# Selective-scan block with mixing and table FFN on one core: where the next group's weights are transposed

## The reference, cut to what matters

```
proj = einsum('bld,pd->blp', h, in_proj_w)            # 10304 x 512 weights
gate, hbc, dt = split(proj)
xBC = silu(causal_conv_4_taps(hbc))
x, B, C = split(xBC)                                  # 64 heads of 64, 8 groups, state 128
state_t = state_{t-1} * dA_t + dt_t*x_t (outer) B_t ; y_t = state_t . C_t     # 32 steps
y  = y + x * D
yn = y * rsqrt(mean(y*y over the 512 channels of a group) + eps) * norm_weight * silu(gate)
out = einsum('bli,di->bld', yn, out_proj_w)           # 512 x 4096 weights
```

## Time and profile before

| | |
|---|---|
| median of 3 runs | 3331.55 us |
| profiled execution, its own time | 3330.75 us |
| its span, first to last instruction | 3329.0 us |
| mean granted TensorE clock | 0.997 |
| TensorE matmuls busy | 3293.0 us (99%) |
| VectorE busy | 2609.7 us (78%) |
| ScalarE busy | 1765.0 us (53%) |
| GpSimd busy | 738.1 us (22%) |
| DMA queue of SP | 464.72 MB, 41.2% of 16 engines |

### The profile page before, as it was taken

One profiled execution on the slowest core, in us unless ns is written; L12 is line 12 of the kernel. 1 busy time (PEld: TensorE's weight loads), 2 busy tenths in 40 slices (PEclk: granted clock), 3 DMA queues, 4 the chain that ended last, 5 costly groups with the idle time before them and its releaser, 6 DMA issues. The chain is left out here.

```text
span 3329.0 us, 86577 instructions
## 1 busy us (share of the span) xinstructions
PE 3293.0 (99%) x33306; PEld 2735.0 (82%) x33306; DVE 2609.7 (78%) x4367; ACT 1765.0 (53%) x3203; POOL 738.1 (22%) x520
## 2 busy tenths in 40 slices
PE   8999999999999999999999999999999999999999
PEld 6778788888888888888888888888888888888888
DVE  6787878888888888888888888888888878887443
ACT  5666665555555555555555555555555545554111
POOL 1122212222212222112222112222122221222333
PEclk9999999999999999999999999999999999999999
DMA  7433354334533364334443363435433542225331
GB/s 276 161 112 114 139 186 161 106 134 168 187 118 126 114 225 140 120 126 169 159 139 137 115 213 109 139 139 180 155 119 120 181 159 79 99 78 157 98 90 60
DMA packets 207793, 466.29 MB, mean 140 GB/s; under 512 B 35134, under 2 KB 80606, under 8 KB 198284
## 3 DMA queue, kind: packets, MB, share of 16 engines
q1 hardware_dynamic: 206364, 464.72, 41.2%
q0 software_dynamic: 368, 0.85, 0.1%
q10 hardware_dynamic: 1024, 0.27, 0.0%
HBM read 313.68 MB, written 152.09 MB: 140 GB/s over the span
## 5 line engine op out<-in xcount | busy, mean ns | idle before, releaser
L1155 PE MATMUL low_banks<-ht,wt 128*128 128x512 f32 x6144 | 1423.4, 390 | 9.3 <-DVE xc L1404 9.3
L1155 PEld LDWEIGHTS low_banks<-ht,wt 128*128 128x128 f32 x6144 | 1153.6, 188 | 258.6 <-DVE xc L1404 13.1
L1404 DVE SCALAR_TENSOR_TENSOR xc<-low_banks,cvw,xc 128x496 f32<-128x496 f32 (+2 forms) x1152 | 824.0, 717 | 221.1 <-ACT xc L1294 193.2
L1250 PE MATMUL bank<-wot,gy 128*128 128x512 f32 x3072 | 729.7, 393 | 1.2 <-DVE gy L1446 1.2
L1250 PEld LDWEIGHTS bank<-wot,gy 128*128 128x128 f32 x3072 | 567.2, 188 | 129.1 <-DVE wnext L1440 10.6
L1294 ACT ACTIVATE xc<-low_banks,cvb,cvw 128x512 f32<-128x512 f32 x384 | 298.6, 780 | 497.6 <-PE low_banks L1155 497.5
L1092 POOL TENSOR_TENSOR r<-rv,neg_half 128x4 f32<-128x4 f32 x64 | 98.4, 1537 | 1767.2 <-DVE rv L1494 1767.2
L1155 PE MATMUL bank<-ht,wt 128*128 128x512 f32 x1536 | 387.3, 401 | 0.0
L1155 PEld LDWEIGHTS bank<-ht,wt 128*128 128x128 f32 x1536 | 280.2, 189 | 55.8
L1073 POOL TENSOR_TENSOR segr<-adts,mask_le 128x1024 fp32r<-128x1024 f32 x128 | 243.1, 1921 | 351.8 <-DVE adts L1395 351.8
L1273 ACT ACTIVATE xc<-xc 128x512 f32<-128x512 f32 x384 | 241.1, 628 | 140.1 <-DVE xc L1404 139.4
(11 more groups left out here) (195 smaller groups left out, 3444.4 us busy)
## 6 DMA issues: line engine op xcount, KB each, us to landing
ht<-h_d SPq DMA_DIRECT2D x63, 2048.0 KB, 8.9
acc_d<-acc SPq DMA_DIRECT2D x64, 1024.0 KB, 4.3
wt_d<-wnext SPq DMA_DIRECT2D x112, 512.0 KB, 9.4
acc<-acc_d SPq DMA_DIRECT2D x56, 1024.0 KB, 7.0
wt<-wt_d SPq DMA_DIRECT2D x70, 512.0 KB, 6.6
stage<-in_L_attn_in_proj_w SPq DMA_DIRECT2D x84, 256.0 KB, 2.7
wot<-wt_d SPq DMA_DIRECT2D x28, 512.0 KB, 8.0
xb<-in_x SPq DMA_DIRECT2D x8, 1024.0 KB, 8.4
```

Source lines behind the costliest of these rows:

```text
L1155: ins = pe.matmul(pb[:, :], wt[:, n, l, k, :], ht[:, rr, k, :], start=(q == 0 and k == 0), stop=(q == 2 and k == KC - 1))
L1250: ins = pe.matmul(bank[OUT[t]][:, :], gy[:, c, l, t * P:(t + 1) * P], wot[:, rr, c, :], start=(c == 0 and q == 0), stop=(c == CT - 1 and q ...
L1404: ins = dve.scalar_tensor_tensor(dst, src, cvw[:, n, TAPS - 1 - k:TAPS - k], dst, ALU.mult, ALU.add)
```

## The change

The next group's weights are no longer transposed by TensorE. In pass `it`, ScalarE splits each raw chunk of 512 32-bit numbers a row into two planes of 16-bit halves (`halves`, laid over the part of `gy` that channel tile 2 uses later), SP issues one transposing DMA for each chunk (`turned`, laid over the low parts' place in `wnext`), and in pass `it + 1` GpSimd joins the halves again in `stage`, ScalarE copies the high parts after its first tap, and GpSimd subtracts for the low parts; then SP stores them and loads the next raw chunks. ScalarE may not overwrite `halves` until the DMAs are done, so it waits for them before `high(2)`. The 14 chunks go through in seven passes, and the eighth moves no raw chunk. TensorE has one loop for all groups. In the first group ScalarE's sort of x is gone: VectorE's addition reads x from z at a step of 4 elements.

```diff
@@ line 890 of before @@
+    halves = [nc.alloc_sbuf_tensor_at(f"halves{u}", [P, 2, DM], U16, offset=gy_at + 8 * TT * HG * L + 4 * DM * u) for u in range(2)]
+    turned = [nc.alloc_sbuf_tensor_at(f"turned_halves{u}", [P, 2 * KC, P], U16, offset=sh.wnext_at + 8 * DM * u + 4 * DM) for u in range(2)]
...
@@ line 983 of before @@
-def next_chunks(j):
-    return 2 + j, (j % 2 if j < NBLK - KC else NPJ + j - (NBLK - KC))
 def load_raw(g, j):
-    for u, n in enumerate(next_chunks(j)):
-        sp.dma_start(stage[u][:, :], weight_rows(a, n, g)).then_inc(s_raw[u], 16)
+    for u in range(2):
+        if j < NBLK - 1:
+            sp.dma_start(stage[u][:, :], weight_rows(a, 2 * j + u, g)).then_inc(s_raw[u], 16)
+        else:
+            sp.sem_inc(s_raw[u], 16)
+def store_next(g, j):
+    for u in range(2):
+        if j > 0:
+            sp.dma_start(sh.wt_d[ds(g, 1), 2 * (j - 1) + u].rearrange("o p n -> p (o n)"),
+                         wnext[:, u, :, :].rearrange("p a n -> p (a n)").bitcast(F32)).then_inc(s_nst, 16)
+        else:
+            sp.sem_inc(s_nst, 16)
+def turn_next(it):
+    sp.wait_ge(s_nst, 32 * it + 64)
+    sp.sem_inc(s_ngo, 1)
+    for u in range(2):
+        sp.wait_ge(s_nsplit, 2 * it + u + 1)
+        sp.sem_inc(s_ngo, 1)
+        sp.dma_start_transpose(turned[u][:, :, :], halves[u][:, :, :].rearrange("p a n -> p (a n)")).then_inc(s_nturn[u], 16)
...
@@ line 998 of before @@
     over = last and j == NBLK - 1
     nxt = g + 1
     turn = j == NBLK - 1 and not last
-    sp.wait_ge(s_accst, 16 * it + 16)
-    if not last:
-        load_raw(nxt, j)
+    def exchange():
+
+        if not last:
+            sp.wait_ge(s_nlo, 2 * it + 2)
+            sp.sem_inc(s_ngo, 1)
+            load_raw(nxt, j)
+            store_next(g, j)
+        sp.wait_ge(s_accst, 16 * it + 16)
+        if not first:
+            sp.dma_start(acc[:, :, :], acc_v[j]).then_inc(s_accin, 16)
+        else:
+            sp.sem_inc(s_ngo, 1)
+
+    if not turn:
+        exchange()
+        if not last:
+            turn_next(it)
     if turn:
         sp.wait_ge(s_nst, 32 * it + 32)
-    if not first:
-        sp.dma_start(acc[:, :, :], acc_v[j]).then_inc(s_accin, 16)
-    if turn:
+        sp.sem_inc(s_ngo, 1)
         for n in range(NPJ - 1):
             sp.wait_ge(s_proj, NPJ * it + n + 1)
             sp.dma_start(wt[:, n, :, :, :].rearrange("p a k n -> p (a k n)").bitcast(F32),
                          sh.wt_d[ds(g, 1), n].rearrange("o p n -> p (o n)")).then_inc(s_wt[n], 16)
+            if n == NCV - 3:
+                exchange()
+            elif n == NCV - 1:
+                turn_next(it)
             if n == NCV:
                 sp.wait_ge(s_conv, NCV * (it + 1))
                 load_conv_params(nxt, sp)
...
@@ line 1028 of before @@
-    if not last:
-        sp.wait_ge(s_nlo, 2 * it + 2)
-        for u, n in enumerate(next_chunks(j)):
-            sp.dma_start(sh.wt_d[ds(g, 1), n].rearrange("o p n -> p (o n)"),
-                         wnext[:, u, :, :].rearrange("p a n -> p (a n)").bitcast(F32)).then_inc(s_nst, 16)
...
@@ line 1065 of before @@
+def join_next(it):
+    for u in range(2):
+        pool.wait_ge(s_nturn[u], 16 * it)
+        pool.sem_inc(s_nready, 1)
+        pool.tensor_copy(stage[u][:, :].bitcast(U16).rearrange("p (n a) -> p a n", a=2),
+                         turned[u][:, :, :].rearrange("p (a k) c -> p a (k c)", a=2)).then_inc(s_njoin, 1)
+def low_next(it):
+    for u in range(2):
+        pool.wait_ge(s_nhi, 2 * it + u + 1)
+        pool.tensor_tensor(wnext[:, u, 1, :], stage[u][:, :], wnext[:, u, 0, :].bitcast(F32),
+                           ALU.subtract).then_inc(s_nlo, 1)
...
@@ line 1126 of before @@
+def scan_pass(g, j, prepare):
+    if prepare:
+        join_next(NBLK * g + j)
     scan_products(g, j)
+    if prepare:
+        low_next(NBLK * g + j)
     decay_products(g, j)
     root(NBLK * g + j)
...
@@ line 1228 of before @@
-    for u in range(2 if prepare else 0):
-        pe.wait_ge(s_raw[u], 16 * it + 16)
-        for k in range(KC):
-            ins = pe.transpose(bank[NEXT[u]][:, k * P:(k + 1) * P], stage[u][:, k * P:(k + 1) * P], sh.ident[:, :])
-        ins.then_inc(s_nps, 1)
...
@@ line 1247 of before @@
-            elif c == 0 and prepare and OUT[t] in NEXT:
-                pe.wait_ge(s_nlo, 2 * it + NEXT.index(OUT[t]) + 1)
-with pe.Fori(0, G - 1) as g:
+with pe.Fori(0, G) as g:
-        attend(g, j, True)
-with pe.Fori(0, NBLK) as j:
-    attend(G - 1, j, False)
+        attend(g, j)
...
@@ line 1297 of before @@
-        if prepare:
-            act.wait_ge(s_nps, 2 * it + u + 1)
-            act.wait_ge(s_nst, 32 * it + 32)
-            act.activation(wnext[:, u, 0, :], bank[NEXT[u]][:, :], ACT.Copy).then_inc(s_nhi, 1)
+        act.wait_ge(s_njoin, 2 * it + u + 1)
+        act.wait_ge(s_nst, 32 * it + 32)
+        act.activation(wnext[:, u, 0, :], stage[u][:, :], ACT.Copy).then_inc(s_nhi, 1)
+    def next_split(u):
+        act.wait_ge(s_raw[u], 16 * it + 16)
+        act.activation(halves[u][:, :, :], stage[u][:, :].bitcast(U16).rearrange("p (n a) -> p a n", a=2),
+                       ACT.Copy).then_inc(s_nsplit, 1)
+    if prepare and not opening:
+        next_high(0)
+        next_high(1)
...
@@ line 1312 of before @@
     tap(NCV - 2)
     silu(NCV - 3)
     tap(NCV - 1)
+    if prepare:
+        next_split(0)
+        next_split(1)
     silu(NCV - 2)
     silu(NCV - 1)
     gate(0)
...
@@ line 1325 of before @@
     gate(2)
     skip(2)
     skip(3)
-    next_high(0)
     high(0)
-    next_high(1)
     square(0)
     gate(3)
     high(1)
     square(1)
+    for u in range(2 if prepare else 0):
+        act.wait_ge(s_nturn[u], 16 * it + 16)
     high(2)
     square(2)
     high(3)
...
@@ line 1344 of before @@
-    if first:
-        act.wait_ge(s_accst, 16 * it + 16)
-        for t in range(TT):
-            act.wait_ge(s_xin[t], 16 * it + 16)
-            act.activation(acc[:, t, :].rearrange("p (r m) -> p r m", r=R), z[:, t, :].rearrange("p (m r) -> p r m", r=R),
-                           ACT.Copy).then_inc(s_xsort, 1)
-with act.Fori(0, NBLK) as j:
-    attend(0, j, True, first=True)
+attend(0, 0, True, opening=True)
+with act.Fori(1, NBLK) as j:
+    attend(0, j, True)
...
@@ line 1436 of before @@
-    def next_low(u):
-        if prepare:
-            dve.wait_ge(s_nhi, 2 * it + u + 1)
-            dve.tensor_tensor(wnext[:, u, 1, :], bank[NEXT[u]][:, :], wnext[:, u, 0, :].bitcast(F32),
-                              ALU.subtract).then_inc(s_nlo, 1)
...
@@ line 1478 of before @@
-    next_low(0)
-    next_low(1)
...
@@ line 1500 of before @@
-    if not first:
+    if first:
+        dve.wait_ge(s_accst, 16 * it + 16)
+    else:
         dve.wait_ge(s_accin, 16 * (it - NBLK) + 16)
 for t in range(TT):
     dve.wait_ge(s_out, TT * it + t + 1)
     if first:
-        dve.wait_ge(s_xsort, TT * it + t + 1)
-    dve.scalar_tensor_tensor(acc[:, t, :], bank[OUT[t]][:, :], r[:, t:t + 1], acc[:, t, :],
+        dve.wait_ge(s_xin[t], 16 * it + 16)
+    def by_remainder(plane):
+        return plane.rearrange("p (r m) -> p r m", r=R)
+    before = z[:, t, :].rearrange("p (m r) -> p r m", r=R) if first else by_remainder(acc[:, t, :])
+    dve.scalar_tensor_tensor(by_remainder(acc[:, t, :]), by_remainder(bank[OUT[t]][:, :]), r[:, t:t + 1], before,
                             ALU.mult, ALU.add).then_inc(s_acc, 1)
```

More of the change, by code:

```diff
@@ L22 @@
 U8 = mybir.dt.uint8
+U16 = mybir.dt.uint16
 ALU = mybir.AluOpType
@@ L897, in attend_part @@
     bank = sh.bank
-    XT, SEG, CB, OUT, SSQ, NEXT = (4, 5, 6, 7), (4, 5), 3, (4, 5, 6, 7), 3, (5, 6)
+    XT, SEG, CB, OUT, SSQ = (4, 5, 6, 7), (4, 5), 3, (4, 5, 6, 7), 3
     scanned = sh.low_banks
     s_raw = [sem(f"s2_raw{u}") for u in range(2)]
-    s_nps = sem("s2_nps")
+    s_nsplit = sem("s2_next_split")
+    s_nturn = [sem(f"s2_next_turned{u}") for u in range(2)]
+    s_ngo = sem("s2_next_turn_may_start")
+    s_nready = sem("s2_next_halves_there")
+    s_njoin = sem("s2_next_joined")
     s_nhi = sem("s2_nhi")
@@ L915, in attend_part @@
     s_xin = [sem(f"s2_xin{t}") for t in range(TT)]
-    s_xsort = sem("s2_x_sorted")
     s_accst = sh.s_accst
@@ L1041, in step @@
                 n = NPJ - 1
-                sp.wait_ge(s_nst, 32 * it + 64)
                 sp.dma_start(wt[:, n, :, :, :].rearrange("p a k n -> p (a k n)").bitcast(F32),
@@ L1108, in gpsimd_part @@
         for s in range(R):
+            join_next(1 + s)
             scan_products(0, 1 + s)
-            pool.wait_ge(s_segr, 2 * s + 6)
-            pool.wait_ge(s_step, s + 2)
+            low_next(1 + s)
+            decay_products(0, 1 + s)
+            pool.wait_ge(s_nlo, 2 * s + 4)
+            pool.wait_ge(s_stepped, SEGB * s + 2 * SEGB)
             rows = slice(s * L, (s + 1) * L)
@@ L1122, in gpsimd_part @@
             pool.wait_ge(sh.s_cbq, spread)
-            decay_products(0, 1 + s)
             root(1 + s)
-        def scan_pass(g, j):
```

(18 more changed lines are left out.)

## The result

The changed kernel took 3293.09 us (median of 4 runs, 3292.65 to 3295.56) against 3331.57 us (3329.17 to 3333.57) for the kernel before: a ratio of 0.9886, 95% interval 0.9872 to 0.9900. The forecast was 3291. The profiled execution took 3293.53 us; its span is 3291.6 us (forecast 3289.3), its mean granted clock 0.998.

The account below looks back on a forecast made before the run. TensorE was taken as the bound, its matmuls filling 99% of the span. Span 3329.0 us less 0.4 (pass 0), 15.9 (first group), 19.9 (passes 8 to 55), 3.5 (loop change) gives 3289.3; plus 1.75 around it, 3291 us; range 3284 to 3340.

Parts of the forecast that it names:

- TensorE's transposes: TensorE, passes with next weights: removing the transposes saves 0.42 us a pass, 19.9 us over passes 8 to 55.
- The last group's pass: TensorE's pass without next weights, taken as model of the changed pass: 45.28 us against 45.70, then waiting for gy.
- The prediction's two rows: Middle pass: transposes take 1.09 us; last group's pass: TensorE idles 0.18 us until VectorE's gy.
- One loop: TensorE at pass 56: one loop instead of two removes the stop read as second-copy code coming in, 3.5 us.
- The first group: First eight passes: 378.15 us become 362.2, saving 15.9 us, of which 3.4 transposes and 12.5 the sort.
- 12.5 the sort: First group: ScalarE's four copies sorting x between passes delay VectorE's residual add; removing them saves 12.5 us.
- The strided read: VectorE reading x at a 16-byte stride, first group: between nothing and 1.9 us more a pass, hidden, taken as 0.
- The added work: GpSimd's joins and low parts, ScalarE's splits and high parts, SP's issues: all beside TensorE, hidden, no cost.
- The first and the third rival: ScalarE's splits take 2.2 us each: 3333 us, chance 0.09; GpSimd's 16-bit copies over 3.3 us each: 3571 us, 0.04.
- The transposing DMAs: SBUF to SBUF, 256 KB each, before ScalarE's high(2) and the load of h: under 5 us each, cost 0.
- the fork: Transposing DMAs from 7.5 us each delay high(2) and h, so it gets slower: 3644 us with 16-byte pieces, chance 0.14.
- the upper bound: Transposing DMA of 256 KB in 2-byte pieces: 131072 packets at 9.6 ns over 16 engines, 79 us.

Follow-up runs that it names:

- four and eight idle transposes: Changed kernel with four or eight unread transposes of the identity added to every TensorE pass: 3292.9 us with four, 3315.86 us with eight.
- the better order: Changed kernel with the output projection's first channel tile reordered, the eight high-part matmuls ahead of the four low-part ones: 3264.42 us, ratio 0.9794.
- the kernel that turns beside the scan: Changed kernel with the transposing DMAs held back until nine projections are done, 28 us into the pass instead of 20: 3306.87 us (one run).
- the kernel whose h came late: Changed kernel with the transposing DMAs held back until all ten projections are done, ahead of the load of h: 3378.11 us median.

## Why the prediction was right, and the step that was not

**TensorE's transposes: right.** 45.70 to 45.30 us a pass. The last group's pass was the right model, for the reason given; four and eight idle transposes show the edge of the wait. The prediction's two rows don't add up by themselves (1.09 us of transposes less 0.18 of idle is not 0.42): from start to start the transposes are 0.85 us, and the wait is 0.44, what the better order gets back. The 0.9 us missing over passes 8 to 55 are 0.02 us a pass. The last group also takes 45.30 in the kernel before with x ahead, so they don't come from the edits; what sets them is open.

**One loop: right, size and cause.** Putting the second copy back brought back the stop, the slow matmuls and the price, and with them the four packets of the instruction queue.

**The first group: the size right, the reason wrong.** The step "12.5 the sort" failed. The 12.5 us came from ScalarE waiting for x behind two stores of 512 KB: with the load moved alone they come back in the kernel before, and with the sort put back they stay away. The row with the idle time and its releaser, 17.7 us `<-DMA z<-in_x`, stood in the prediction and was read for its duration alone. The prediction even noted that x's loads would no longer have the stores ahead of them, and put nothing on it. That the total came out is luck: the change happened to cure the real cause too. Had the change taken the sort away and left the load, by this account little of the 12.5 us would have come; that kernel was not run. The strided read costs VectorE more than the plain add, and it is hidden as assumed: 1.13 against 0.74 us.
```profile
L1555 DVE SCALAR_TENSOR_TENSOR acc<-bank,r,acc 128x512 f32<-128x512 f32 x224 | 152.7, 744 | 9.5 <-POOL r L1141 8.9
...
L1555 DVE SCALAR_TENSOR_TENSOR acc<-bank,r,z 128x512 f32<-128x512 f32 x32 | 34.2, 1133 | 1.4 <-POOL r L1141 1.4
```

**The added work: hidden, and cheaper than taken.** Groups of the changed kernel:
```profile
L1105 POOL COPY stage<-turned_halves 128x1024 uint16<-128x1024 uint16 x110 | 143.4, 1350 | 0.0
...
L1112 POOL TENSOR_TENSOR wnext<-stage,wnext 128x512 fp32r<-128x512 f32 x110 | 140.1, 1295 | 0.0
...
L1349 ACT ACTIVATE halves<-stage 128x1024 uint16<-128x1024 uint16 x112 | 111.6, 1045 | 0.0
```
A join 1.35 us (taken 1.9), a low part 1.30 (at most 1.57), a split 1.05 (1.26). The first and the third rival needed 2.2 and over 3.3 us.

**The transposing DMAs: right side of the fork.** 4.4 us (median) to landing where under 5 was taken and 7.5 would have decided. The window is open less far than the prediction had it, though: not only who waits matters, but the scan, which loses 0.28 us when they run beside it. The 256 KB move in about 1050 packets of some 250 bytes each, neither the single elements nor the small pieces of the upper bound. In the kernel that turns beside the scan the two stand alone in the queue:
```profile
DMA packets 2112, 0.52 MB, mean 119 GB/s; under 512 B 2112, under 2 KB 2112, under 8 KB 2112
...
q1 hardware_dynamic: 2112, 0.52, 61.9%
```
Over the 4.4 us of that stretch the engines are busy 61.9%: 0.619 x 16 x 4.4 us / 2112 = 20.6 ns a packet, against the 9.6 ns that I had put on the smallest ones, and 119 / 0.619 = 192 GB/s while they run. The Trainium skill (VectorE: DVE Perf Modes, section The three transpose paths) gives 1309 ns for one 128x128 block by DMA. As a serial price that was an estimated 21 us for the 16 blocks; the trace does not agree, both DMAs are through in 4.5 us. The Trainium skill's page Advanced Engine Details and Errata, section X-Bar Transpose (TRN2), has transposing DMAs as fast as regular ones, and that comes nearer: in that kernel 256 KB land in 3.2 us, a plain load of 256 KB in 2.8. Its 350 to 400 GB/s were not reached here.

**The rest of the difference, 2.3 us of span.** The first stage ended 1.2 us later (first projection at 110.19 us, before 109.00), 0.02 us a pass make 1.2 us, less 0.1 at the end. The first stage is not in the change's reach: over the kernels here pass 0's root starts between 156.7 and 160.1 us.

## What to carry to other kernels

Before charging an operation's duration to a gap, look at what released the operation: if it was a DMA, the order of issues may be the cure, as it was here, and it can be free. Work taken off the engine that sets the time pays only down to the next wait; look for independent matmuls (here products of the high part) that can stand in that wait, and do both together. When moving a transfer, look at what it will run beside, not only at who waits for it.

## What the runs showed of the hardware

- Two transposing DMAs beside the scan slow its 256 matmuls of 32x32 from 2.74 to 3.02 us; an ordinary load that moves 0.3 MB beside its second half does not. In the changed kernel the transposing DMAs run beside projections and the transposes of x, and no slowing is seen: the latter take 1.97 us as before.
- A transposing DMA of 256 KB of 16-bit data holds SP 1.3 us for its issue and lands 3.2 us (median) after it when little else moves, 4.4 us when the load of `acc` goes out 5 us ahead of it; in the kernel that moved that load behind it, it is 3.2 again.
- TensorE's first walk through a copy of its loop cost 2.06 us of stop in the middle of a scan in the copy put back (2.16 in the kernel before, 2.00 at the loop's first entry in the changed one), with packets of some 16 KB on an instruction queue around it, and 1.4 us more behind the stop (12 matmuls in 4.46 us instead of 3.02), where the granted clock was 0.59, so partly at 1.2 GHz instead of 2.4.
- In the kernel whose h came late, TensorE had stood 4.8 us; the granted clock was 0.67 from 486.5 to 491 us, so partly at 1.2 GHz, and 1.00 again from 491 to 499 us, and the 48 matmuls of the stretch took 12.52 instead of 11.09 us.
- Reading 32-bit numbers at a step of 16 bytes cost VectorE 1.13 instead of 0.74 us for 512 of them, and ScalarE 1.11 instead of 0.63. The Trainium skill (SBUF — State Buffer, section Door 1: The DMA port swizzle) has SBUF in lines of 16 bytes, with a penalty for each access that crosses to a new line, and gives 4 fp32 as how far one can stride for free. A step of 4 fp32 takes a new line each time, and in these rows it is not free.
